# Output products directly behind the scores, ahead of the transposes of probabilities

## What is computed

```python
c_q = hidden_states @ w_q_down
c_kv = hidden_states @ w_kv_down                     # 64 wide, shared by the 32 heads
q_lat = einsum('bhsd,hdr->bhsr', q_nope, wuk)
scores = einsum('bhsr,btr->bhst', q_lat, c_kv) + einsum('bhsd,btd->bhst', q_rope, k_rope[:, 0])
probs = softmax(where(causal, scores / sqrt(DN + DR), min))
out_lat = einsum('bhst,btr->bhsr', probs, c_kv)
out = einsum('bhsr,hdr->bhsd', out_lat, wuv).transpose(0, 2, 1, 3).reshape(b, s, H * DV)
return out @ w_out

x = x + 0.5 * ffn(layernorm(x))
x = x + attn(layernorm(x))
x = x + 0.5 * ffn(layernorm(x))
```

## Time and profile before

| | us |
|---|---|
| runs shown, median of 3 | 1338.89 |
| lowest, highest | 1338.37, 1340.07 |
| the profiled execution | 1338.54 |
| its span, first to last instruction | 1336.6 |
| TensorE matmuls busy | 1200.8 |
| VectorE busy | 849.3 |
| ScalarE busy | 638.9 |
| GpSimd busy | 513.5 |

### The profile page before, as it was taken

One profiled execution on the slowest core, in us unless ns is written; L12 is line 12 of the kernel. 1 busy time (PEld: TensorE's weight loads), 2 busy tenths in 40 slices (PEclk: granted clock), 3 DMA queues, 4 the chain that ended last, 5 costly groups with the idle time before them and its releaser, 6 DMA issues.

```text
span 1336.6 us, 27786 instructions
## 1 busy us (share of the span) xinstructions
PE 1200.8 (90%) x8424; PEld 1013.3 (76%) x8424; DVE 849.3 (64%) x3266; ACT 638.9 (48%) x1810; POOL 513.5 (38%) x821
## 2 busy tenths in 40 slices
PE   3587899999988799999989699999989789999996
PEld 3465788888777688888768678888869678888876
DVE  1564666667667566676667466676666666666755
ACT  1433555555413455555513365555532365555641
POOL 0311544444312454444422254444430254544430
PEclk8798999999989899999989899999998899999998
DMA  9251000000000000000010000000010000000000
GB/s 270 84 154 59 1 1 1 0 0 2 33 24 10 3 2 1 0 0 1 2 32 33 3 1 1 0 0 1 1 33 33 1 1 1 1 0 0 2 1 32
DMA packets 21232, 27.64 MB, mean 21 GB/s; under 512 B 9942, under 2 KB 11734, under 8 KB 20474
## 3 DMA queue, kind: packets, MB, share of 16 engines
q1 hardware_dynamic: 16922, 17.98, 4.2%
q10 hardware_dynamic: 4192, 8.19, 2.1%
HBM read 21.97 MB, written 4.19 MB: 20 GB/s over the span
## 4 chain that ended last, share of the span: by engine, by line
PE 67%; issue 15%; DVE 10%; ACT 3%; POOL 2%; DVEq 0%; POOLq 0%; ACTq 0%
PE Y L932 12%; PE Y L906 10%; PE XZ L891 9%; PE Y L840 8%; PE XZ L870 5%; PE Y L747 5%; PE XZ L872 4%; PE XZ L871 4%; PE XZ L747 3%; PE Y L852 3%; PE XZ L720 1%; PE Y L793 1%; DVE small L1342 1%; DVE qT_lo L1290 1%; DVE XZ L1342 1%
## 5 line engine op out<-in xcount | busy, mean ns | idle before, releaser
L701 POOL TENSOR_TENSOR prob<-prob,small 128x512 f32<-128x512 f32 (+3 forms) x512 | 361.3, 722 | 433.9 <-DVE small L1297 432.9
L1342 DVE CUSTOM_DVE_ANT_0 XZ<-XZ,mask 128x512 f32<-128x512 f32 (+3 forms) x512 | 244.3, 508 | 286.4 <-issue 283.3
L1078 ACT ACTIVATE prob<-XZ,small 128x512 f32<-128x512 f32 (+3 forms) x512 | 267.1, 526 | 288.4 <-DVE small L1342 288.3
L870 PE MATMUL XZ<-kT_hi,qT_hi 128*128 128x512 f32 (+3 forms) x512 | 186.9, 365 | 25.4 <-DVE qT_lo L1290 14.9
L891 PE MATMUL XZ<-ident,prob 128*128 128x128 f32 x1280 | 195.6, 275 | 0.2
L872 PE MATMUL XZ<-kT_hi,qT_lo 128*128 128x512 f32 (+3 forms) x512 | 166.8, 326 | 0.0
L871 PE MATMUL XZ<-kT_lo,qT_hi 128*128 128x512 f32 (+3 forms) x512 | 166.2, 325 | 0.0
L891 PEld LDWEIGHTS XZ<-ident,prob 128*128 128x128 f32 x1280 | 147.6, 140 | 21.1 <-POOL prob L701 7.3
L906 PE MATMUL Y<-probT,ckv 128*64 128x384 f32 (+2 forms) x1280 | 152.3, 384 | 8.7 <-ACT probT L596 8.0
L596 ACT ACTIVATE probT<-XZ 128x512 f32<-128x512 f32 x192 | 114.8, 598 | 79.5 <-PE XZ L891 77.2
L906 PEld LDWEIGHTS Y<-probT,ckv 128*64 128x64 f32 x1280 | 84.0, 136 | 71.5 <-issue 44.9
(11 more groups left out here) (203 smaller groups left out, 2512.5 us busy)
## 6 DMA issues: line engine op xcount, KB each, us to landing
wout_nat<-in_L_attn_w_out_dram SPq DMA_DIRECT2D x8, 1024.0 KB, 5.9
out_dram<-x_sb SPq DMA_DIRECT2D x16, 256.0 KB, 2.0
x_next<-_attn_hidden_states_dram SPq DMA_DIRECT2D x12, 256.0 KB, 3.1
nope_a<-_L_attn_w_q_up_nope_dram ACTq DMA_DIRECT2D x2, 1024.0 KB, 14.1
wbase_nat<-in_L_ffn_W_base_dram ACTq DMA_DIRECT2D x1, 1024.0 KB, 5.5
nope_b<-_L_attn_w_q_up_nope_dram ACTq DMA_DIRECT2D x2, 512.0 KB, 13.1
rope_a<-_L_attn_w_q_up_rope_dram ACTq DMA_DIRECT2D x1, 1024.0 KB, 10.7
rope_bb<-_L_attn_w_q_up_rope_dram ACTq DMA_DIRECT2D x2, 512.0 KB, 13.1
```

The lines of the kernel that those rows point to most:

```text
L701: last = nc.gpsimd.tensor_tensor(prob[u % RING][:, c:c + w], prob[u % RING][:, c:c + w], inv_sum[:, u % RING, m:m + 1].broadcast_to([P, w] ...
L870: nc.tensor.matmul(bank[:, c:c + w], high, kT_hi[:, 0:w], start=True, stop=False)
L1078: last = nc.scalar.activation(prob[u % RING][:, c:c + w], score_ps[u % 2][:, c:c + w], ACT.Exp, bias=neg_max[:, u % RING, m:m + 1], scale= ...
L1342: last = nc.vector.tensor_tensor_reduce(bank, bank, mask[:, S - w:S], -1.0, HIGHEST, ALU.add, ALU.min, neg_max[:, u % RING, m:m + 1])
```

## The change

In the slots in which TensorE has an output group, that group now stands directly behind the scores (and, where there are any, the query products) and ahead of the transposes. In the 26 such slots of a batch with scores, and in the two behind them, O and T thereby change places. The slots with `pv` have no output, so its place against O doesn't change. No instruction is added or taken away, and the instructions of the other engines and their order are the same.

```diff
@@ -957,12 +957,12 @@
                         n = BODY_PAIRS * g + p + 1
                         if k in (0, 2) and queries:
                             q_products(b, n, k // 2, False)
+                        if output_rows(u) is not None and known(g, u, 3 * UNITS):
+                            output(b, g, p, output_rows(u))
                         if k == PV_SLOT and known(g, u, UNITS):
                             pv(b, g, p - 1)
                         if known(g, u, T_LAG) and within(g, u, SLOTS - 1 + T_LAG):
                             transpose_probs(b, g, u - T_LAG)
-                        if output_rows(u) is not None and known(g, u, 3 * UNITS):
-                            output(b, g, p, output_rows(u))
                         if k in (1, 3) and queries:
                             q_transposes(b, n, k // 2, False)
```

## The result

| | before | after |
|---|---|---|
| median, us | 1339.16 (4 runs) | 1356.55 (4 runs) |
| lowest, highest | 1338.37, 1340.07 | 1353.34, 1357.54 |
| the profiled execution | 1338.54 | 1355.94 |
| its span | 1336.6 | 1354.0 |
| TensorE matmuls busy | 1200.8 | 1202.7 |

The ratio is 1.0125, with a 95% interval from 1.0107 to 1.0144: 17 us slower, where 15.4 was forecast (1354.0 us, against a median of 1356.55). TensorE's busy time is the same to 2 us, so the time is waits.

The account below looks back on a forecast made before the run. TensorE's own work, matmuls busy 90% of the span, was taken as the bound. Steady part 0, last pair 1.13 plus batch end 2.73 make 3.86 us; 4 x 3.86 = 15.4 us on 1338.54 gives 1354.0 us, range 1346 to 1364.

Parts of the forecast that it names:

- The mechanism: VectorE's in-order queue: the copy waits for both TensorE groups and the addition queues behind it; VectorE free 1.2 us later, formerly 0.6.
- Steady part, slot 2: VectorE, free at 889.33, just meets its maximum, due 889.38 at the earliest; cost taken as 0, at worst 2.6 us.
- the tie: Steady pairs, slot 2: VectorE is free only 0.05 us before its maximum may start.
- Steady part, slot 1: Output group of every second pair, waiting for VectorE's 0.3 us late rounding rest: cost 0, bounds 0 to 4.8 us.
- the gap of 0.59: Steady pairs, slot 1: time from VectorE's late rounding rest to the scores' end, said to cover the 0.24 us start.
- Last pair: Slot 1 of a batch's last pair: late output group delays VectorE's maximum and the probability-value product by 1.13 us a batch.
- End: Behind a batch's last scores: two output groups held by additions, last product held by ScalarE's copy; 2.73 us a batch.
- Sum: Whole kernel: 3.86 us a batch over four batches, 15.4 us slower, 1354.0 us.
- The clock: Rival at the end of a batch: three new waits lower the clock, 3.4 us a batch, 1367.8 us; chance 0.05.
- the three waits: New TensorE waits at the end of a batch, ahead of two output groups and the last probability-value product.
- VectorE as gate of the steady part: Rival: steady pairs lose time in slots 2 and 1, 8 to 10 us more, about 1363 us; chance 0.17.
- The gain on GpSimd's side: Rival, faster: later transposes recover 7.3 us of weight loads put down to GpSimd's scaling, 1331.2 us; chance 0.04.

Follow-up runs that it names:

- the first four: Changed kernel with part of the exchanges undone, against the kernel before: end only 1.0096, all but the end 1.0046, steady part only 1.0022, slot 76 only 1.0025.

## Why the prediction was right

- **The mechanism** held: additions behind copies in VectorE's queue. The first rival of the experiments (a cost of each exchange) fell with the first four, and the two kernels that took the mechanism away, VectorE adding first and banks of their own for the last two groups, took most of the loss with it.
- **Steady part, slot 2**: the tie. Copy 0.03 us after T, maximum 0.05 after its scores. Right.
- **Steady part, slot 1**: taken as 0, with up to 0.2 us each. It is the term that was sized wrong: S lost 0.39 us a batch, 1.2 us in all, within the bound of 4.8. In the pair shown, two errors of 0.1 met: the copy in slot 4 starts 0.12 us after T and not 0.03, so VectorE is 0.4 late and not 0.3; and from oT_lo to the first product it is 0.39 us in the steady part, not 0.24 as in the last pair. And the gap of 0.59 was counted to the end of the scores, while a group that isn't held starts its first product 0.16 us before that (861.46 and 861.62), with its weight load at 861.34, 0.12 earlier still. Of the gap some 0.4 were there to use, and 0.09 and 0.15 more were asked of it: the first product came 0.04 us late and, being held, took 0.50 instead of 0.39. Not every such group loses that: in the chain of the third batch the six add 1.39, 1.44, 1.53, 1.44, 1.52 and 1.38, which is 0.4 us over 1.38 each.
- **Last pair**: 1.13 forecast, 1.23 to 1.28 measured. The same 0.09 of the copy is the difference. Of it, 0.43 comes from slot 74 and 0.85 from slot 76; the prediction had 0.3 and 0.8.
- **End**: 2.73 forecast, 2.81 measured, with every link in place. O(81) was due 986.19 - 982.98 = 3.21 us after the scores and came after 3.30; O(82) 6.69 and 6.77; PV 9.47 and 9.55.
- **Sum**: 15.4 forecast, 17.4 in the span. The missing 2.0 are 1.2 in the steady part, 0.5 in the last pairs and 0.3 in the ends. All three go the same way, so no error hid another. The median of 1356.55 stands 0.6 above the profiled execution.
- **The rivals.** The clock didn't fall: in the ten us with the three waits (1.03, 1.38 and 0.69 us, ahead of O(81), O(82) and PV) TensorE was busy 3.97 and 2.93 of 5 us, and the granted clock stayed at 1.00 (first two rows); it fell to 0.57 in 1017 to 1025 (third row), as at the same place of the program before. That such short waits bring the clock down was the rival's guess: these three didn't, and the 3.4 us a batch at which it was priced did not come.

```profile
995.00:1000.00 5.00, 3.97 (x24) 3.15 (x22) 2.73 (x9) 1.99 (x6) 2.37 (x4) 1.00 0.68 209
1000.00:1005.00 5.00, 2.93 (x17) 1.88 (x16) 2.94 (x5) 0.60 (x1) 0.00 (x0) 1.00 0.01 4
...
1017.00:1025.00 8.00, 6.19 (x31) 6.16 (x31) 5.08 (x21) 1.58 (x4) 0.92 (x2) 0.57 0.00 0
```

- VectorE as gate of the steady part came true only in this 1.2 us. What the prediction held against it, starts that are regular to 0.05 us, isn't so in the changed kernel: the start of VectorE's copy varies by 0.09 and TensorE's start behind oT_lo by 0.15. The gain on GpSimd's side did not come: the weight loads' 7.3 us of the earlier trace rows are 7.0 now, and no stretch got shorter by them. On the path lay the 0.3 us of T(78) at the end of a batch, which the prediction had already counted.

```profile
L891 PEld LDWEIGHTS XZ<-ident,prob 128*128 128x128 f32 x1280 | 149.2, 140 | 26.9 <-POOL prob L701 7.0
```

## What to carry to other kernels

When two groups change places on one engine, look at the queue of the engine that serves both: if it keeps the old order, the result that is now early waits behind the one that is now late, and the loss is not a switch on the first engine but both services in series (here copy and addition, 1.30 us from 1000.28 to 1001.58). In a steady part with slack such an exchange is nearly free (1.2 us in all here, inside the steady part); price it where the work that hid it runs out, at the last pair and behind the last scores (1.2 and 2.8 us a batch here), and count the links there one by one. And where a wait is held by one copy, ask what stands ahead of that copy in its own engine's queue.

## What was not expected of the hardware

The start after a release is not one number. VectorE's copy starts 0.03 us after TensorE's transposes in one slot and 0.12 in another, and the chain shows its sequencer (DVEq, line 594) in between in the second case: there a register instruction of 0.04 us carries the wait for the transposes, in the first case the copy carries it itself, with nothing of line 594 ahead of it (T ends at 868.62, the copy starts at 868.65). Slot 74 of the changed kernel, where T ends at 982.45 and the copy starts 0.11 later:

```profile
982.45 0.03 issue
982.47 0.04 DVEq L594
982.51 0.04 issue
982.56 0.07 DVE probT L598
```

TensorE's first product starts 0.23 us after oT_lo in the last pair and up to 0.39 us after it in the steady part. Between the sequencer's wait for oT_lo (line 920, 985.17) and the first weight load (985.36) stands one register instruction (line 922, 0.03 us) in the last pair, and the weight load carries the wait for the addition itself; in the steady part (866.18 and 866.52) that of line 922 takes 0.07 us, and a second one (line 932, 0.05 us), which makes that wait, stands there too. That these instructions of the sequencers are the reason was not tried by itself. In a place with 0.05 us to spare, such a tenth (0.12 against 0.03) decides.
